# A depthwise-convolution mixer stage: zero padding, 64-column products, regrouped transposes, a deeper pipeline and half-image taps

## The reference, cut to what matters

```python
h = _layernorm(x, n1_g, n1_b)
p = h @ w_in + b_in                                   # 96 -> 192 channels
local = conv_general_dilated(p, k_conv, (1, 1), 'SAME',   # depthwise, 3 x 3
                             feature_group_count=inner)
lr, rl = _ema_scan(local, axis=2), _ema_scan(local, axis=2, reverse=True)
tb, bt = _ema_scan(local, axis=1), _ema_scan(local, axis=1, reverse=True)
mixed = 0.25 * (lr + rl + tb + bt) + local
mixed = _layernorm(mixed, on_g, on_b)                 # over the 192 channels
x = x + (mixed @ w_out + b_out)                       # 192 -> 96 channels
```

## Time and profile before

| what | value |
|---|---|
| median of 3 runs | 1211.01 us (1208.01 to 1211.23) |
| profiled execution, its own time | 1204.52 us |
| span of its trace | 1202.7 us |
| PE busy, LDWEIGHTS busy | 1083.8 us (90%), 708.1 us (59%) |
| DVE busy, ACT busy, POOL busy | 702.9, 525.4, 395.2 us |
| mean granted TensorE clock | 0.962 of full |
| the stage `conv_mixer` in the trace | 210.7 us to 341.2 us |

### The profile page before, as it was taken

The page is one execution under the profiler, slowest core; times in us unless marked ns, Lnnn a source line. Parts: engine busy times, 40 slices in busy tenths (PEclk is TensorE's granted clock), DMA queues, the critical chain, the costliest instruction groups (busy, mean ns, idle before and its releaser), DMA issues. The chain is left out here.

```text
span 1202.7 us, 26997 instructions
## 1 busy us (share of the span) xinstructions
PE 1083.8 (90%) x10561; PEld 708.1 (59%) x10561; DVE 702.9 (58%) x2003; ACT 525.4 (44%) x855; POOL 395.2 (33%) x616
## 2 busy tenths in 40 slices
PE   5999988899989799999999996888888978899998
PEld 2677655577745567676666664455455444466665
DVE  3899734687734466666666666476455565443333
ACT  1666623466523333434343331454343422365654
POOL 4766553766364310110101111425000000336442
PEclk9999999899979899999999999888799999899999
DMA  6400000000000000000000000000000000000000
GB/s 124 88 2 2 2 2 0 1 1 2 1 1 1 1 1 1 1 2 1 1 1 1 1 1 1 1 1 2 2 2 1 2 2 2 1 8 15 9 15 14
DMA packets 28534, 9.50 MB, mean 8 GB/s; under 512 B 26689, under 2 KB 28416, under 8 KB 28416
## 3 DMA queue, kind: packets, MB, share of 16 engines
q1 hardware_dynamic: 25392, 6.95, 2.8%
q10 hardware_dynamic: 3024, 0.92, 0.4%
HBM read 6.29 MB, written 1.57 MB: 7 GB/s over the span
## 5 line engine op out<-in xcount | busy, mean ns | idle before, releaser
L164 POOL TENSOR_TENSOR ln_v<-MV,eps 128x2 f32<-128x2 f32 (+3 forms) x81 | 16.2, 200 | 407.9 <-PE bank L1141 244.7
L1203 ACT ACTIVATE fa_e<-bank 128x1024 f32<-128x1024 f32 x64 | 65.5, 1023 | 156.8 <-PE bank L1111 156.8
L1255 DVE TENSOR_REDUCE fa_z<-bank 128x4 f32<-128x1024 f32 x64 | 77.9, 1217 | 26.4 <-PE bank L1093 24.4
L137 PE MATMUL bank<-hT,e_w 96*64 96x512 f32 x384 | 91.0, 610 | 0.0
L2049 ACT ACTIVATE ex_G<-bank,e_b 128x512 f32<-128x512 f32 x96 | 64.4, 687 | 49.9 <-PE bank L137 47.2
L2121 DVE SCALAR_TENSOR_TENSOR X<-bank,ex_L,X 128x96 f32<-128x96 f32 x128 | 31.7, 310 | 91.5 <-PE bank L137 85.0
L1853 DVE TENSOR_REDUCE ca_z<-bank 128x2 f32<-128x256 f32 x96 | 48.9, 551 | 48.7 <-PE bank L1580 48.7
L137 PEld LDWEIGHTS bank<-e_w,ex_G 128*64 128x64 f32 x1536 | 67.0, 137 | 17.3 <-issue 10.6
L1111 PE MATMUL bank<-fa_a,fa_b 64*128 64x256 f32 x512 | 73.0, 404 | 1.1 <-DVE fa_a L1262 1.1
L1771 ACT ACTIVATE ca_e<-bank 128x768 f32<-128x768 f32 x48 | 38.9, 810 | 76.4 <-PE bank L1580 76.4
L167 POOL TENSOR_TENSOR ln_r<-ln_v,minus_half 128x2 f32<-128x2 f32 (+3 forms) x81 | 71.8, 886 | 0.0
(11 more groups left out here) (251 smaller groups left out, 2493.7 us busy)
## 6 DMA issues: line engine op xcount, KB each, us to landing
out_tokens<-X SPq DMA_DIRECT2D x8, 192.0 KB, 2.1
X<-in_x SPq DMA_DIRECT2D x14, 96.0 KB, 3.4
e_w<-in_L_ffn_w SPq DMA_DIRECT2D x2, 576.0 KB
bias0r<-in_L_conv_rpb_table ACTq DMA_DIRECT2D x16, 24.0 KB
m0w<-in_L_conv_mlp_w SPq DMA_DIRECT2D x2, 144.0 KB
m1w<-in_L_conv_w SPq DMA_DIRECT2D x2, 144.0 KB
f_w<-in_L_ffn_W SPq DMA_DIRECT2D x2, 142.5 KB
mixer<-in_mixer SPq DMA_DIRECT2D x1, 256.0 KB
```

The lines of the kernel that those rows point to most:

```text
L137: last = pe.matmul(out[columns], weights[:, columns], moving, **flags)
L1203: act.activation(E[v % 2][:], k.banks[:, b:b + 2, :].rearrange("p i (c q) -> p i c q", c=2), ACT.Exp).then_inc(s["exp"], 1)
L1255: dve.tensor_reduce(Z[v % 2][:].rearrange("p c (i d) -> p i c d", i=2)[:, :, :, D2], k.banks[:, b:b + 2, :].rearrange("p i (c q) -> p i c ...
```

## The change

- `Z` gets 256 columns in place of 192, and columns 192 to 255 are zeros; the group 1 half of `ZT` starts as zeros. So `back` transposes four full 128 x 128 blocks and `out` contracts over 128 rows for both groups. POOL clears both ahead of the grids.
- `mix`, `out` and `widen` are issued through `halves`. `taps` was already 64 columns wide.
- A PE turn is now `conv_t(n-1)`, `tokens(n+1)`, `back(n-3)`, `mix(n-1)`, `taps(n)`, `widen(n+1)`, `out(n-3)`: the full-width instructions first, then the 64-column ones. `back` and `out` run one image later, so four images are in flight, and the loop has one more turn.
- An ACT turn is now: `cm_loc` copy of image n-1, `tokens(n+1)`, `zt(n-3)`, `normalised(n-2)`, copy of taps(n), `widened(n+1)`.
- DVE does each tap as two instructions of eight image rows each (128 x 128 elements). Each waits for the instruction two before it, not the one before. The residual of image n-4 is added after tap 0, its statistics stand after tap 2, `norm2(n-1)` after tap 5.

```diff
-        Z = sb("z", [P, 2, CI])
+        Z = sb("z", [P, 2, 2 * P])
+        TAPS = 2 * 9
@@ gpsimd
                 norm(0, 0)
+                pool.memset(Z[:, :, CI:2 * P], 0.0)
+                pool.memset(ZT[:, 1, :, :], 0.0)
                 for i in range(2):
                     last = pool.memset(grid[i][:], 0.0)
@@ tensor: mix, back, out, widen
-                            last = pe.matmul(mixed[n % 2][:, t * CI:(t + 1) * CI], k.mixer[:, j, t * P:(t + 1) * P], loc[:, j, :],
+                            last = halves(pe, mixed[n % 2][:, t * CI:(t + 1) * CI], k.mixer[:, j, t * P:(t + 1) * P], loc[:, j, :],
-                            last = pe.transpose(bank[5][0:part[j], (2 * j + t) * P:(2 * j + t + 1) * P], Z[:, t, j * P:j * P + part[j]], k.ident[:])
+                            last = pe.transpose(bank[5][:, (2 * j + t) * P:(2 * j + t + 1) * P], Z[:, t, j * P:(j + 1) * P], k.ident[:])
-                            last = pe.matmul(bank[6][:, t * C:(t + 1) * C], ZT[0:part[j], j, t, :], k.wout[0:part[j], j, :],
+                            last = halves(pe, bank[6][:, t * C:(t + 1) * C], ZT[:, j, t, :], k.wout[:, j, :],
-                        last = pe.matmul(bank[1][:, j * TOK:(j + 1) * TOK], k.win[:, j * P:(j + 1) * P], k.hT[slot][:, 0:TOK], start=True, stop=True)
+                        last = halves(pe, bank[1][:, j * TOK:(j + 1) * TOK], k.win[:, j * P:(j + 1) * P], k.hT[slot][:, 0:TOK], start=True, stop=True)
@@ tensor: the loop
-                for n in range(IMAGES + 2):
+                for n in range(IMAGES + 3):
                     slot = n % 2
+                    if 1 <= n <= IMAGES:
+                        conv_t(n - 1, 1 - slot)
                     if n + 1 < IMAGES:
                         tokens(n + 1, 1 - slot)
+                    if n >= 3:
+                        back(n - 3)
                     if 1 <= n <= IMAGES:
                         mix(n - 1)
-                    if n >= 2:
-                        back(n - 2)
                     if n < IMAGES:
                         taps(n, slot)
                     if n + 1 < IMAGES:
                         widen(n + 1, 1 - slot)
-                    if n >= 2:
-                        out(n - 2)
-                    if n < IMAGES:
-                        conv_t(n, slot)
+                    if n >= 3:
+                        out(n - 3)
@@ vector
+                def body(n, slot):
                     dve.wait_ge(s["p"], n + 1)
                     after(dve, s["ct"], n - 1)
+                    o = acc[slot][:].rearrange("p (h i c) -> p h i c", h=2, c=SIDE)
                     for tap in range(9):
+                        if tap == 1 and n >= 4:
+                            residual(n - 4)
+                        if tap == 3 and n >= 4:
+                            statistics(dve, k, s, n - 4, 2)
+                        if tap == 6 and n >= 1:
                             norm2(n - 1)
                         y, x = divmod(tap, 3)
                         kk = k.kconv[:, 0, tap:tap + 1]
+                        for h in range(2):
+                            top = y + h * SIDE // 2
+                            src = grid[slot][:, 0, top:top + SIDE // 2, x:x + SIDE]
+                            if tap == 0:
+                                dve.tensor_scalar(o[:, h], src, kk, None, ALU.mult).then_inc(s["conv"], 1)
+                            else:
+                                dve.wait_ge(s["conv"], TAPS * n + 2 * tap + h - 1)
+                                dve.scalar_tensor_tensor(out=o[:, h], in0=src, scalar=kk, in1=o[:, h], op0=ALU.mult, op1=ALU.add).then_inc(s["conv"], 1)
```

More of the change, by code:

```diff
@@ L948, in normalised @@
                     for t in range(2):
-                        last = act.activation(Z[:, t, :], mixed[n % 2][:, t * CI:(t + 1) * CI], ACT.Identity, bias=o2[:, t, :], scale=r2[:, t, :])
+                        last = act.activation(Z[:, t, 0:CI], mixed[n % 2][:, t * CI:(t + 1) * CI], ACT.Identity, bias=o2[:, t, :], scale=r2[:, t, :])
                     last.then_inc(s["z2"], 1)
@@ L963, in _ @@
                 widened(0, 0)
-                for n in range(IMAGES + 2):
+                for n in range(IMAGES + 3):
                     slot = n % 2
-                    if n >= 2:
-                        normalised(n - 2)
+                    if 1 <= n <= IMAGES:
+                        act.wait_ge(s["ct"], n)
+                        after(act, s["mix"], n - 1)
+                        act.activation(loc[:], bank[2][:, 0:2 * CI].rearrange("p (t c) -> p t c", t=2), ACT.Copy).then_inc(s["loc"], 1)
                     if n + 1 < IMAGES:
                         tokens(n + 1, 1 - slot)
-                    if n >= 2:
-                        zt(n - 2)
+                    if n >= 3:
+                        zt(n - 3)
+                    if 2 <= n <= IMAGES + 1:
+                        normalised(n - 2)
                     if n < IMAGES:
@@ L1000, in residual @@
                     dve.wait_ge(s["xb"], n + 1)
-                    add_and_stats(dve, k, s, n, 2, bank[6][:, 0:2 * C].rearrange("p (t c) -> p t c", t=2))
-                def body(n, slot, first, last):
+                    add_new(dve, k, s, n, 2, bank[6][:, 0:2 * C].rearrange("p (t c) -> p t c", t=2))
+                def body(n, slot):
                     dve.wait_ge(s["p"], n + 1)
                     after(dve, s["ct"], n - 1)
-                    o = acc[slot][:].rearrange("p (i c) -> p i c", c=SIDE)
+                    o = acc[slot][:].rearrange("p (h i c) -> p h i c", h=2, c=SIDE)
@@ L1014, in body @@
                         kk = k.kconv[:, 0, tap:tap + 1]
-                        if tap == 0:
-                            dve.tensor_scalar(o, src, kk, None, ALU.mult).then_inc(s["conv"], 1)
-                        else:
-                            after(dve, s["conv"], 9 * n + tap)
-                            dve.scalar_tensor_tensor(out=o, in0=src, scalar=kk, in1=o, op0=ALU.mult, op1=ALU.add).then_inc(s["conv"], 1)
-                in_turn(IMAGES, body)
-                residual(IMAGES - 3)
@@ L1022, in _ @@
-                norm2(IMAGES - 1)
-                residual(IMAGES - 2)
-                residual(IMAGES - 1)
+                        for h in range(2):
[6 more added lines that the diff above has]
+                                dve.scalar_tensor_tensor(out=o[:, h], in0=src, scalar=kk, in1=o[:, h], op0=ALU.mult, op1=ALU.add).then_inc(s["conv"], 1)
@@ L1027, in centre_weights @@
+                for n in range(IMAGES):
+                    body(n, n % 2)
+                for n in range(IMAGES - 4, IMAGES):
+                    if n == IMAGES - 3:
+                        norm2(IMAGES - 1)
+                    residual(n)
+                    statistics(dve, k, s, n, 2)
 def centre_weights(pool, k, s):
```

16 lines of the change are left out of this document (4 added, 12 removed).

## The result

The changed kernel takes 1199.49 us (median of 4 runs, 1195.03 to 1200.68) against 1210.44 for the kernel before: a ratio of 0.9906, with a 95% interval of 0.9877 to 0.9936. Timed a second time beside other kernels it was 1199.41 us, ratio 0.9928 (0.9906 to 0.9950). That is 9 to 11 us faster. The forecast was 1197.5, 13.5 us faster, in a range of 1191 to 1205.

What follows compares the result with a forecast made beforehand. PE's own list and one 0.36 us gap were taken to bound the 7.17 us turn. +0.5 - 2.8 - 9.7 - 0.3 - 1.2 = -13.5 us, from the median 1211.01 to 1197.5, range 1191 to 1205.

Steps and rivals of the forecast that it cites:

- the path over two turns: From conv_t(n) to image n+2's opening, 7.26 falls to 6.48; then DVE's body: two turns take 6.53 + B.
- the MLP's pairs: 64-column matmuls of the MLP stage, 0.083 us a pair; eight pairs bring out on PE from 1.46 to 0.66.
- back off the path: On PE, back moves ahead of mix into the 0.36 us gap, so its 0.53 us leaves the path.
- Taps in halves: On DVE, halves follow each other at 0.236 us, bounds 0.205 and 0.27; a tap costs 0.47 against 0.51.
- the pair in SBUF: Two 96-element DVE STTs with SBUF inputs, the first holding the engine 0.17; gives 0.205 for 128 elements.
- B: In sums, DVE's body, 6.04 us. As rival: padding does not help, out stays 1.46, 1201.5 us, chance 0.09.
- The start: First images of the stage: clears cost +0.5 us, image 1 still opens at 222.41, image 4 opens 2.8 sooner.
- rival D: PE idles over 0.4 us a turn and its clock is lowered, or stages behind meet it; 1208 us, chance 0.05.
- The end: End of the stage: out(15) falls from 2.75 to 1.5 us, -1.2; the last body is 0.3 shorter.
- A: Halves do not overlap on DVE, each costs 0.35 us; the turn is 7.9, the kernel slower, 1221; chance 0.07.
- C: DVE halves at 0.27, B = 6.6, T = 6.6, 1202 us; or at 0.205, 1193 us; chance 0.12 each.
- T: The stage's period per turn, forecast at 6.29 us against 7.17, saving 0.88 a turn over 11 turns.

Runs made afterwards that it cites:

- whole-image taps: The changed kernel with each tap again as one instruction of 256 elements: 1193.44 us, ratio 0.9889 to the kernel before.
- the filled wait: The changed kernel with 16 bf16 matmuls of 256 columns on PE ahead of the first conv_t: 1200.31 us, ratio 0.9934 to the kernel before.
- the padding experiment: The kernel before with the zero padding of Z and ZT and nothing else: 1201.5 us, ratio 0.9955.
- the two padding kernels: The kernel before with the padding alone, 1201.5 us, ratio 0.9955, and with mix, widen and out in halves on top, 1203.18 us, ratio 0.9967.
- only out in halves: The changed kernel with whole-image taps and with mix and widen full width again: 1196.0 us, ratio 0.9897 to the kernel before.
- back behind mix: The changed kernel with back again after mix on PE, the depth kept: 1212.52 us, ratio 1.0036 to the kernel before.
- half-image taps alone: The kernel before with the half-image taps and nothing else: 1213.99 us, ratio 1.0072.

## Why the prediction was right, and where it was off

*What bounds.* Right: PE's list and its gap before, the path over two turns and DVE's body after. The path was forecast at 6.48 from conv_t to the second next opening and is 272.44 - 265.99 = 6.45. With the body of 6.64 the two-turn rule gives (6.45 + 0.05 + 6.64) / 2 = 6.57, and the body alone, less the overlap of 0.05 with the next opening, gives 6.59; in the changed kernel both bind together. The forecast had the path bind and DVE idle.

*out.* Forecast 0.66 by the MLP's pairs. From out's start to its last matmul's is 0.83 less about 0.25, 0.58, and a pair more makes 0.66. End to end it is 1.53 before, 1.03 with the padding alone and 0.83 with the halves: 0.5 of the 0.7 comes from not alternating between 128 and 64 rows.

*Order.* back off the path: forecast 0.53 and the gap. Right, and the largest part: the new order with its one more image in flight, without padding and halves, gives the stage as much as the whole change.

*Taps in halves: the term that was mis-sized.* I took 0.236 a half between bounds of 0.205 and 0.27. Measured 0.26: the upper bound, from the tap's own duration, was the nearer row, and I leaned to the pair in SBUF. Two halves are 0.52, what a whole tap costs. Fifteen spacings make 0.4 us, the first tap in halves 0.39 where I had 0.30, the long half tap beside POOL another 0.12 in the turn shown and 0.16 in most others, which I had not seen at all: B = 6.64 in place of 6.04. Period 6.60 in place of 6.29, 11 x 0.31 = 3.4 us of the forecast gain.

*The start: the step that failed.* I forecast images 0 to 4 to open 2.8 us sooner. They opened 2.4 us later in relation to image 0 (28.9 against 26.5). I wrote that image 1 still opens at 222.41 and that mix(0) starts at 223.14 as before, which means a first body no longer than the old one, and I took 5.1 us for each body before image 4. But beside POOL's first norms the first body took 6.66 us (5.51 before, 5.61 with whole-image taps), image 1 opened at 223.55 and mix(0) started at 225.04, PE waited 2.00 for DVE, and the clock fell, twice. Of the 5.2 us between forecast (23.7 from image 0 to 4) and measurement (28.9), 3.1 are the clock, by the experiment with the filled wait, and 2.1 the longer bodies. The low clock stood in my sum with nothing; I had named it as rival D, for turns in which PE idles more than 0.4 us.

*The end.* Forecast -1.2 and -0.3; from the opening of image 15 to the next stage it is 20.3 before (321.55 to 341.83) and 17.5 now (318.45 to 335.91), -2.8: out(15) and mix(15) met the high clock. In the kernel before the granted clock is 0.50 from 330 to 332 us and from 338 to 340; in the changed one it is 1.00 from 316 us to the stage's end.

*The sum.* Stage: +0.3 (first opening) + 2.4 - 6.3 (72.6 against 78.9 for eleven intervals) - 2.8 = -6.4, where I had -13.5. The whole kernel gained 9 to 11. What lies outside the stage, 3 to 5 us, is not explained: in other kernels of this study with the same code behind the stage, full attention took 352 to 357.5 us. It made the total look better than my sum was. That the measured time fell within the range is in part luck: in the stage, where the sum was made, less than half of the forecast gain came.

*The rivals.* A did not happen: halves do start 0.08 before the last one ends, with waits on DVE's own semaphore too.
The Trainium skill, "VectorE: DVE Perf Modes", "The DRAIN you can't avoid", says that the next operation does not start until the pipe is empty, and that one which is not held (made to wait for all earlier ones) starts earlier. I had set only the first half beside A; the trace agrees with the second, since 0.34 us instructions stand 0.26 apart. Fewer operations were the better choice all the same, as the whole-image taps show.
B is refuted by the padding experiment. C, halves at 0.27 with B = 6.6, T = 6.6 and 1202 us, is the case that came, and I gave it 0.12. D came in part, and not where its condition pointed: in the steady turns PE idles 0.85 us a turn, twice the 0.4 that I had thought risky, and the clock is granted in full from 241.8 to 320 us.

## What to carry to other kernels

When a loop runs over two slots, write down the path from one engine's step to the same slot two turns on, beside each engine's own list: it gave 6.81 and 6.83 for the two padding kernels (6.87 measured in most turns) and 6.6 for only out in halves (6.62), and it told that a shorter out would bring nothing more in the old order. It was no better than the body put into it: with back behind mix and with half-image taps alone the bodies were longer than assumed, and so was the period. Splitting an instruction to hide its wait pays only if the halves stand closer than half the dependent spacing, so take the price from the instruction's own duration less the overlap, not from a shorter relative in another shape. And sum the first turns separately: there a slower DVE lets PE run dry, and in this kernel the clock then took back 3.1 us of the 6.3 that the steady turns earned.

## What the hardware did that I had not expected

POOL and DVE slow each other. With whole-image taps, the tap that starts while POOL's line 173 runs takes 0.70 us in place of 0.485 (mean of 10), and line 173, which itself starts 0.03 after another tap, takes 0.87 in place of 0.59. In the changed kernel line 173 starts beside no tap and keeps its 0.59; the half tap that starts during it takes 0.51 in place of 0.34 (mean of 11). In the kernel before line 165 starts during a tap: it takes 0.72 in place of the 0.50 it has with whole-image taps, and the tap keeps its 0.485. In all four cases the instruction that starts second pays and the first does not; why is not shown.
The Trainium skill, "GPSIMD Engine Reference", Specifications, says that POOL shares its SBUF interfaces with VectorE and lists instructions with two SBUF inputs among those that contend. The traces agree for the taps, which have two inputs in SBUF, and the sum for a body has to say which POOL instruction lies beside which tap, and which starts first.

In the changed kernel two waits of 2.0 us on PE at the start of a stage were each followed by the lower clock, and filling the first with matmuls that compute nothing kept the clock. But the length of one wait does not decide. With whole-image taps a wait of 1.00 us was not followed by a fall; with the padding alone one of 0.98 at the same place was (mix(0) 2.72). With padding and halves 1.53 at the first image was not, and 1.38 at the second was. In the filled kernel a wait of 1.98 before the third image's conv_t (at 236.40) was not, where the changed kernel's 2.01 was. What tells these cases apart stays open. What the filled kernel gained at the start it partly gave back to a low clock at the end.
